# Every second probability tile of an attention kernel is transposed on VectorE with cross-partition DMAs instead of on TensorE

## The reference

```
scores  = (Q K^T) / sqrt(8)                  # 2 x 16 heads x 512 x 512
scores  = conv over keys (3 taps), mixing all 16 heads; + conv_b
weights = softmax(scores)
x       = x + (weights V) Wo^T + bo
```

## Time and profile before

| | |
|---|---|
| runs, us | 269.82, 270.06, 270.51 |
| profiled execution, first to last instruction | 268.3 us (the page gives no other time of it) |
| TensorE busy | 258.0 us (96%) |
| VectorE | 214.0 us (80%) |
| ScalarE | 165.2 us (62%) |
| GpSimd | 142.3 us (53%) |
| chain that ended last | TensorE 82%, VectorE 10%, GpSimd 4% |
| granted clock of TensorE | full throughout |
| DMA | 8.11 MB, nearly all in the first 33 us |

### The profile page before, as it was taken

How to read it: one execution, slowest core, us unless ns; L and a number is a source line. 1 busy time by engine, 2 the same in 40 slices (tenths; PEclk the granted TensorE clock), 3 DMA queues, 4 the chain that set the end, 5 groups by cost and what they waited for, 6 DMA issues and landing times.

```text
span 268.3 us, 5678 instructions
## 1 busy us (share of the span) xinstructions
PE 258.0 (96%) x1835; PEld 191.3 (71%) x1835; DVE 214.0 (80%) x524; ACT 165.2 (62%) x292; POOL 142.3 (53%) x166
## 2 busy tenths in 40 slices
PE   8996989999999999999999999999999999999994
PEld 7455766777777677777667667777676766779982
DVE  2559997988889798888968999889888975686553
ACT  2743887768676776866683577777767771314321
POOL 1029988678687867768482667687863100000000
PEclk9999999999999999999999999999999999999999
DMA  7992000000000000000000000000000000000002
GB/s 222 370 418 85 2 1 1 4 0 0 0 0 0 0 0 0 2 1 2 0 0 2 0 2 0 2 2 0 0 0 0 2 0 2 0 0 4 0 2 78
DMA packets 2964, 8.11 MB, mean 30 GB/s; under 512 B 258, under 2 KB 1794, under 8 KB 2690
## 3 DMA queue, kind: packets, MB, share of 16 engines
q1 hardware_dynamic: 2514, 7.22, 7.2%
q10 hardware_dynamic: 432, 0.65, 0.7%
HBM read 7.34 MB, written 0.52 MB: 29 GB/s over the span
## 4 chain that ended last, share of the span: by engine, by line
PE 82%; DVE 10%; POOL 4%; issue 2%; ACT 1%; DVEq 0%; POOLq 0%; ACTq 0%
PE tp L902 18%; PE sc L777 12%; PE pvbank L794 10%; PE sc L778 9%; PE sc L779 9%; DVE Pb L515 3%; PE sc L993 3%; PE tp L1003 3%; PE sc L721 2%; PE misc L815 2%; DVE PT L631 1%; PE sc L739 1%; PE sc L953 1%; DVE kc L459 1%; PE sc L954 1%
## 5 line engine op out<-in xcount | busy, mean ns | idle before, releaser
L319 ACT ACTIVATE Pb<-Pb,nbias 128x512 f32<-128x512 f32 x128 | 90.7, 721 | 51.5 <-DVE Pb L515 51.0
L515 DVE TENSOR_SCALAR_CACHE_REDUCE Pb<-sc,col 128x512 f32<-128x512 f32 x128 | 93.6, 744 | 19.0 <-PE sc L779 18.3
L902 PE MATMUL tp<-cst,Pb 128*128 128x128 f32 x512 | 76.9, 273 | 0.9 <-DVE PT L631 0.8
L902 PEld LDWEIGHTS tp<-cst,Pb 128*128 128x128 f32 x512 | 63.0, 140 | 20.4 <-issue 1.7
L777 PE MATMUL sc<-Kh,Ql 128*128 128x512 f32 x124 | 60.7, 490 | 0.9 <-POOL Kl L216 0.9
L216 POOL TENSOR_TENSOR Kl<-kc,Kh 128x512 fp32r<-128x512 f32 x29 | 37.5, 1294 | 37.9 <-ACT Kh L314 37.7
L778 PE MATMUL sc<-Kl,Qh 128*128 128x512 f32 x124 | 49.2, 397 | 0.0
L779 PE MATMUL sc<-Kh,Qh 128*128 128x512 f32 x124 | 49.0, 396 | 0.0
L631 DVE COPY PT<-tp 128x512 f32<-128x512 f32 x64 | 43.9, 685 | 1.0 <-PE tp L902 1.0
L228 POOL TENSOR_TENSOR td<-ta,tc_ 128x512 f32<-128x512 f32 x31 | 42.0, 1356 | 2.6
L361 ACT ACTIVATE PT<-tp 128x512 f32<-128x512 f32 x64 | 37.4, 585 | 3.2 <-PE tp L902 2.4
(11 more groups left out here) (232 smaller groups left out, 259.7 us busy)
## 6 DMA issues: line engine op xcount, KB each, us to landing
w1s<-in_w SPq DMA_DIRECT2D x1, 2048.0 KB, 9.6
w2s<-in_w SPq DMA_DIRECT2D x1, 2048.0 KB, 14.0
cst<-in_consts SPq DMA_DIRECT2D x1, 648.0 KB, 5.1
xTs<-in_xT SPq DMA_DIRECT2D x2, 256.0 KB, 3.0
we<-in_wexp SPq DMA_DIRECT2D x2, 256.0 KB, 3.4
b2s<-in_b2row SPq DMA_DIRECT2D x1, 512.0 KB, 14.8
out<-PT SPq DMA_DIRECT2D x2, 192.0 KB, 2.1
wq<-in_wqkvo ACTq DMA_DIRECT2D x1, 320.0 KB, 3.7
```

Source lines behind the costliest of these rows:

```text
L319: act.activation(Pb[:, k, :], Pb[:, k, :], ACT.Exp, bias=nbias[:, k:k + 1], scale=-1.0)\
L515: dve.tensor_scalar(Pb[:, k, :], SC[k % 4][:, :], cb, None, ALU.subtract, ALU.min, accum_out=nbias[:, k:k + 1]).then_inc(s["mx"], 1)
L902: mm = pe.transpose(TP[u % 2][:, k * 128:(k + 1) * 128], Pb[:, u % RING, k * 128:(k + 1) * 128], ident)
```

## The change

In every pair of heads the four even units of each head pair are no longer transposed on TensorE:

- VectorE transposes the tile of `Pb` by blocks of 32x32 (`dve.transpose`) into `TB`, and signals `tb`. `TB` lies in the place of `w2s`, so `w2s` is loaded only behind the last output product, and `b2s` before it.
- A block now has its right content but lies on the wrong group of 32 partitions. When a pair's four block transposes are done, SP issues 16 DMAs (partition group i to partition group i2) from `TB` to `PTB`, 32 partitions x 4 x 128 elements each, with the semaphore `tm0` or `tm1` of that pair.
- Odd units stay on TensorE, now in both banks `tp` in turn, and ScalarE copies them to `PTA`.
- The output product of a pair runs in one piece, nine units behind the pair's last even unit: at unit 15 and at unit 7 of the next group. So the copy of `PV`, `by_token` and the normalisation move to units 8 and 9, `TURN` to 10 and the stages of sequence 0 by some four units.
- The second half of the very last group goes through TensorE in all its units; VectorE copies the even ones to `PTX`. The first of the two last products moves behind the last unit, and the wait for `zlo` ahead of the first dispatch.
- The maximum waits for the transposes of the unit whose slot it takes (`tp` or `tb`), since even units are no longer seen by TensorE.
- In sequence 1 the loops over groups are written out.

```diff
-TURN = 6
+TURN = 10
-AT_DVE = {(0, 2): 12, (0, 11): 3, (0, 14): 6, (1, 0): 1, (1, 1): 7, (1, 5): 8, (NG - 1, 6): 9, (NG - 1, 8): 10,
-          (NG - 1, 10): 5}
+AT_DVE = {(0, 6): 12, (0, 15): 3, (1, 2): 6, (1, 4): 1, (1, 5): 7, (1, 9): 8, (NG - 1, 10): 9, (NG - 1, 12): 10,
+          (NG - 1, 14): 5}
...
+        PTA = flat[:, 0:half].rearrange("p (g k c) -> p g k c", g=G, k=QT)
+        PTB = flat[:, half:2 * half].rearrange("p (w k i c) -> p w k i c", w=2, k=QT, i=4)
+        TB = w2s[:, :, :, :].rearrange("p e j c -> p (e j c)").rearrange("p (w k i c) -> p w k i c", w=2, k=QT, i=4)
...
@@ block.sync
+            sp.dma_start(b2s[:, :], b2row).then_inc(s["b2"], 16)
+            def cross(pair, w):
+                sp.wait_ge(s["tb"], 4 * pair + 4)
+                sp.wait_ge(s["pv"], pair)
+                for i in range(4):
+                    for i2 in range(4):
+                        sp.dma_start(PTB[32 * i2:32 * i2 + 32, w, :, i, :], TB[32 * i:32 * i + 32, w, :, i2, :])\
+                            .then_inc(s[f"tm{w}"], 16)
+            with sp.Fori(0, B * NG - 1) as g:
+                for w in range(2):
+                    cross(2 * g + w, w)
+            cross(2 * (B * NG - 1), 0)
+            sp.wait_ge(s["pv"], 4 * NG + 2)
             sp.dma_start(w2s[:, :, :, :], w2).then_inc(s["w2"], 16)
-            sp.dma_start(b2s[:, :], b2row).then_inc(s["b2"], 16)
...
@@ vector, unit
-                    if u == 4:
+                    if u == 8:
                         raw_out(b, g)
-                    elif u == 5:
+                    elif u == 9:
                         normalise(b, g)
+                    if u % 2 == 1 and (not isinstance(g, int) or n >= 5):
+                        dve.wait_ge(s["tp"], U // 2 * (NG * b + g) + u // 2)
+                    elif u % 2 == 0 and (not isinstance(g, int) or n >= 4):
+                        dve.wait_ge(s["tb"], U // 2 * (NG * b + g) + u // 2 - 1)
                     maximum(n + AHEAD, m % RING, G * g + m // QT - (H if over else 0))
-                if u % 2 == 0:
-                    dve.wait_ge(s["tp"], n + 2)
-                    dve.tensor_copy(PT[:, j % G, :, (u % QT) * 128:(u % QT + 1) * 128],
...
+                elif u % 2 == 0:
+                    if u % (2 * QT) == 0 and (not isinstance(g, int) or b + g > 0):
+                        dve.wait_ge(s[f"tm{w}"], 256 * (NG * b + g))
+                    dve.wait_ge(s["ex"], n + 2)
+                    at = 64 * (j % 2) + 32 * half_tile
+                    dve.transpose(TB[:, w, :, :, at:at + 32].rearrange("p k i c -> p (k i) c"),
+                                  Pb[:, u % RING, :].rearrange("p (k c) -> p k c", c=32)).then_inc(s["tb"], 1)
...
@@ tensor
-            def outputs(hd, j, gi, tiles):
-                pe.wait_ge(s["evd"], 2 * hd + 5)
-                pe.wait_ge(s["eva"], 2 * hd + 5)
+            def outputs(pair, w, gi):
+                pe.wait_ge(s["eva"], 4 * pair + 5)
+                pe.wait_ge(s[f"tm{w}"], 256 * gi + 256)
...
+                            x = PTA[:, 2 * w + i, k, :] if f else \
+                                PTB[:, w, k, :, 64 * i:64 * i + 64].rearrange("p i (t c) -> p t i c", t=2)
...
+                if u == U // 2 - 1 and not (isinstance(g, int) and b + g == 0):
+                    outputs(2 * gi - 1, 1, gi - 1)
+                elif u == U - 1:
+                    outputs(2 * gi, 0, gi)
...
-            for u in range(TURN, U):
-                if u == U - 1:
-                    last_outputs(0)
-                unit(1, NG - 1, u)
+            last_outputs(0)
```

More of the change, by code:

```diff
@@ L169, in build, with last_pair @@
         block = ctx.enter_context(nc.Block())
+        def last_pair(b, g, u):
+            return b == B - 1 and isinstance(g, int) and g == NG - 1 and u >= U // 2
         @block.sync
@@ L367, in unit @@
                     high_half(hd + 2, (u // QT) % 2)
-                if u == 5:
+                if u == 9:
                     stage_values(b, g)
@@ L388, in _ @@
                 unit(0, NG - 1, u)
-            for u in range(U + TURN):
+            for u in range(NG * U):
                 unit(1, u // U, u % U)
-            with act.Fori(1, NG - 1) as g:
-                for u in range(TURN, U + TURN):
-                    unit(1, g + u // U, u % U)
-            for u in range(TURN, U):
-                unit(1, NG - 1, u)
             for k in (0, 2, 3, 4, 5):
@@ L649, in _ @@
                 unit(0, 0, u)
-            with dve.Fori(0, NG - 1) as g:
+            with dve.Fori(0, NG - 2) as g:
                 for u in range(TURN, U + TURN):
                     unit(0, g + u // U, u % U)
-            for u in range(TURN, U):
-                unit(0, NG - 1, u)
+            for u in range(TURN, 2 * U):
+                unit(0, NG - 2 + u // U, u % U)
             dve.wait_ge(s["cst"], 16)
-            for u in range(U + TURN):
+            for u in range(NG * U):
                 unit(1, u // U, u % U)
[L658 to L662, removed]
             def spread(e, b):
@@ L898, in unit @@
                     scores(n + AHEAD, H * b + G * g + m // QT, b + 1 if over else b, m)
-                pe.wait_ge(s["ex"], n + 2)
-                pe.wait_ge(s["evd" if u % 2 == 0 else "eva"], (U // 2) * gi + u // 2 + 1)
-                for k in range(QT):
-                    mm = pe.transpose(TP[u % 2][:, k * 128:(k + 1) * 128],
-                                      Pb[:, u % RING, k * 128:(k + 1) * 128], ident)
-                mm.then_inc(s["tp"], 1)
-                if u % (2 * QT) in (1, 3) and not (isinstance(g, int) and b + g == 0 and u < QT):
-                    outputs(H * b + G * g + u // QT - 2, (u // QT - 2) % G, gi - (1 if u < QT else 0),
-                            (0, 1) if u % QT == 1 else (2, 3))
-                if u == 4 and not (isinstance(g, int) and b + g == 0):
+                odd = U // 2 * gi + u // 2
+                if u % 2 or last_pair(b, g, u):
+                    pe.wait_ge(s["ex"], n + 2)
+                    if last_pair(b, g, u):
+                        bank = TP[u % 2]
+                        if u % 2 == 0 and u > U // 2:
+                            pe.wait_ge(s["evx"], (u - U // 2) // 2)
+                        else:
+                            pe.wait_ge(s["eva"], odd + u % 2)
+                    else:
+                        bank = TP[u // 2 % 2]
+                        if not isinstance(g, int) or odd > 0:
+                            pe.wait_ge(s["eva"], odd)
+                    for k in range(QT):
+                        mm = pe.transpose(bank[:, k * 128:(k + 1) * 128],
+                                          Pb[:, u % RING, k * 128:(k + 1) * 128], ident)
+                    mm.then_inc(s["tp" if u % 2 else "tpx"], 1)
+                if u == U // 2 - 1 and not (isinstance(g, int) and b + g == 0):
+                    outputs(2 * gi - 1, 1, gi - 1)
+                elif u == U - 1:
+                    outputs(2 * gi, 0, gi)
+                if u == 8 and not (isinstance(g, int) and b + g == 0):
                     by_token(b, g)
@@ L939, in _ @@
                 unit(0, NG - 1, u)
-            for u in range(U + TURN):
+            for u in range(NG * U):
                 unit(1, u // U, u % U)
-            with pe.Fori(1, NG - 1) as g:
-                for u in range(TURN, U + TURN):
-                    unit(1, g + u // U, u % U)
-            for u in range(TURN, U):
-                if u == U - 1:
-                    last_outputs(0)
-                unit(1, NG - 1, u)
+            last_outputs(0)
             def dispatch(t, h):
@@ L960, in _ @@
             pe.wait_ge(s["mx"], U * NG * B + 1)
+            pe.wait_ge(s["zlo"], 1)
             dispatch(0, 0)
```

54 lines of the change are left out of this document (31 added, 23 removed).

## The result

The changed kernel takes 278.7 us (median of 4 runs, 276.59 to 283.44), the kernel before beside it 270.28 us (269.82 to 272.49): ratio 1.026, 95% interval 1.019 to 1.033. Forecast were 260.5 us, with a range up to 274. Runs more than 1.5% above the fastest of their kernel, here that of 283.44 us, are left out of the ratios and intervals; the medians are over all runs. The span of the profiled execution is 276.4 us, where 258.7 was forecast.

The account below looks back on a forecast made before the run. TensorE was taken to bound the kernel before. Stretch gains of 11.15 us, less 1.0 for the tail and 0.55 for meeting bounds, gave 9.6: span 258.7, with 1.8 more for the median 260.5 us; range 255 to 274.

Parts of the forecast that it names:

- the DMA sum: SP's 16 DMAs per pair: 15 issue steps of 0.46 us plus 2.0 us landing, 8.9 us, 9.0 with wake-up.
- D: Time from a pair's last block transpose to the landing of its DMAs, with wake-up: forecast 9.0 us.
- the ring: Per group, D, output product, restart and scores, then VectorE to the next last block transpose: 20.6 us, hidden under 21.9.
- rival 2: The pair's DMAs land late: their ring takes over at D 10.3 us, the change loses at D 12.05; chance 0.16.
- The clock costed at nothing: TensorE, busy 19.7 of 22 us per group, was expected to lose no time to a change of clock.
- Start: Stretch up to the first RAW copy at 57.46 us: a gain of 0.8 us, bounded by 0 and 2.4.
- TensorE freed: Half the transposes (3.5 us) and two restarts (0.4 us) leave TensorE, leaving it 19.7 us per group.
- rival 1: VectorE's block transpose is slow and makes VectorE the bound, past 1.03 us each; 282.5 us at 1.2; chance 0.12.
- rival 3: The small transfers do not overlap: 32 us per pair, 64 us per group, over 500 us; chance 0.02.
- The `kc` ring: Single `kc` buffer: VectorE waits for GpSimd's Kl behind ScalarE's Kh, 0.48 us per head; bounds the group at 21.9 us.
- Rival 4: VectorE's block transposes hold up GpSimd's port, Kl 0.44 us later per head: group 23.45 us, total 269; chance 0.08.
- Tail: From the last RAW copy to the end, products and dispatches stand one behind the other: a loss of 1.0 us.

Follow-up runs that it names:

- twelve DMAs: The changed kernel without the four of 16 DMAs per pair that stay within the same 32 partitions, leaving old data there: 261.32 us, ratio 0.964 to the kernel before.
- the best kernel: The changed kernel with four of a pair's 16 DMAs issued by ScalarE and two `kc` buffers: 260.49 us, ratio 0.956 to the kernel before.

## Why the prediction was wrong

- **The step that failed is a term of the DMA sum**: "issues follow each other at 0.46 to 0.48 us", "whatever they carry". Measured 0.644. D is 11.9 us and not 9.0, the ring 23.5 and not 20.6, and so above 21.9. This was rival 2's mechanism, at a pitch of 0.66 us from which it "decides against the change"; it stood at a chance of 0.16 on the ground that "nothing queues here". That ground was true and didn't bear: the issue is dear by itself. The earlier trace rows were all issues out of HBM, and the change's go from SBUF to SBUF. The sensitivity was in the text ("every 0.1 us of a slower issue takes 1.5 of that"), the margin was 1.3 us, and the price of one operation had been read off another kind of it. In the earlier trace rows, L187's 0.81 us should have widened the range. By that ring alone the change would only have gained nothing; that it lost 3% is in the next two points and the tail.
- **The clock costed at nothing**: wrong. Three products took 3.39, 2.76 and 3.26 us in place of 1.93, 3.6 us in all, part of it on the path. Two of them stand behind 3.4 and 3.6 us of waiting for DMAs; the third, of 2.76 us, behind a wait for VectorE's `diag`, which the change with twelve DMAs has too (2.12 us, then 2.82 us of product).
- **Start**: a gain of 0.8 us was forecast. The change's first RAW copy is 4.7 us late against the forecast, that of the twelve DMAs still 2.1. In the change the first product begins 12.2 us behind its last block transpose (38.98 + 0.70 to 51.85) and runs at the low clock.
- **TensorE freed**: right, 19.1 to 20.0 us against 19.7. **Block transpose**: right, 0.703 us against 0.69, and rival 1 falls. **VectorE**: right, 20.8 to 21.1 against 20.9. The estimate of 0.71 from the Trainium skill (VectorE: DVE Perf Modes, the three transpose paths) agrees with the trace; the figure there is for bf16, the tiles here are fp32.
- **Landing of 64 KB**: right, 2.1 us, overlapped; rival 3 falls. The Trainium skill's rule to join small transfers, as under 64 KB one pays mostly overhead (DMA: Bandwidth & Descriptors, rules for kernel authors), points the right way for these of 64 KB: 9.7 of the 11.9 us of D are issues one behind the other. What costs here is the issue and not the 2.1 us of landing, by which I had weighed the rule.
- **The `kc` ring**: right in place, and hidden. L479 waits for Kl 16 times; with the DMAs in time the group is 21.7 to 22.3 us against 21.9.
- **Rival 4, GpSimd's port**: L246, as L223 before, has a mean of 1074 ns, 3.7% above before's 1036, and a median of 1124 against 1122. With the DMAs in time a quiet group is 21.7 to 22.3 us and not this rival's 23.45.
- **w2 free**: right. Issued at 233.40, landed 8.8 us later, first needed at 248.9. **Tail**: right, 57.6 us against 57.3.
- **A reading without effect**: "the L777 behind it 0.43 in place of 0.23". From one start to the next, the L777 behind the half product takes 0.34 us (65.79 to 66.13) and the next one, behind transposes, 0.32; the restart of 0.2 us stands ahead of the product, which starts 0.53 us behind its transposes where L777 starts 0.36 behind them. The sum of 1.20 us for a half product holds.

What stays open. Why an issue out of SBUF costs 0.60 us behind another, and only 0.465 alone, is measured and not explained. The clock's share of the 8 us was not isolated. The stretch with sequence 0's stages (29.7 us in the change, 29.5 with twelve DMAs, 27.6 in the best kernel, 26.9 forecast) is at clock 0.94, 0.94 and 1.00. TensorE's wait for `diag` there is 2.14, 2.12 and 0.96 us, and the product behind it takes 2.76, 2.82 and 1.93. That fits a loss by the clock which the late DMAs do not cause, but no run changes the clock alone there.

## What to carry to other kernels

When an operation is split into many small DMAs, the price to read is that of the issue, of the same kind (source and destination), in a row and not alone; times their number it stands on the path of whoever waits for the last. If no row of the trace shows that kind, the term is unknown, and a margin of 6% over a ring, here 1.3 us, is no margin. And where a change frees the bound, look at every ring that comes near the new period: here three of them (20.6, 20.9, 21.9 by the forecast) stood within 1.3 us, and curing one (issues on ScalarE) lengthened another (`kc`), until both were eased.

## What the hardware showed that was not expected

- SP's issue: 0.43 us out of HBM, 0.465 us out of SBUF alone, 0.60 us out of SBUF in a row, the same for 32, 128 or 512 pieces within 8%. On ScalarE's queue 0.62 us in the median.
- 12.6 MB of SBUF-to-SBUF traffic (192 x 64 KB) beside the kernel before did not change its time (ratio 0.9999, 0.996 to 1.004).
- A product of 32 matmuls took 1.93 us at the 2.4 GHz level and 3.26 to 3.39 us after 3.4 to 3.6 us of idle time on TensorE, the granted clock being 0.64 in the 4 us from 52 us. After 2.58 us it took 1.94.
